# One written-out order of the calls on each engine of a two-layer sequence kernel, and its last batch without matmuls that nothing reads

## The reference, cut to what matters

```
# layer 0, per batch: linear attention over the context, then batch norm and a residual
g, theta, phi = conv1x1(g_w, ctx), conv1x1(theta_w, x), conv1x1(phi_w, ctx)
y = (theta^T phi / 512) g ;  x1 = bn(w_w y + w_b) + x
# layer 1, per batch: time mixing with a recurrence over 256 steps in 32 heads of 16
xa = ln(x1);  sx = shift(xa) - xa;  five mixes xw, xk, xv, xr, xg through low-rank tanh
w = exp(-exp(time_decay + tanh(xw d1) d2));  r, k, v = xr Wr^T, xk Wk^T, xv Wv^T;  g = silu(xg Wg^T)
s_new = k v^T + w * s;   out = r (faaaa * k v^T + s)      # step by step in time
x2 = x1 + (groupnorm(out) * g) Wo^T
# then channel mixing
xc = ln(x2); xk2, xr2 from xc and its shift
out = x2 + sigmoid(xr2 fWr^T) * (square(relu(xk2 fWk^T)) fWv^T)
```

## Time and profile before

| what | value |
|---|---|
| median of three runs | 872.42 us (869.52 to 874.44) |
| span of the profiled execution | 871.9 us |
| PE matmul busy | 813.5 us, 93% |
| VectorE busy | 602.6 us, 69% |
| ScalarE busy | 354.4 us, 41% |
| GpSimd busy | 295.4 us, 34% |
| mean granted TensorE clock | 0.986 |

### The profile page before, as it was taken

One profiled execution on the slowest core, in us unless ns is written; L12 is line 12 of the kernel. 1 busy time (PEld: TensorE's weight loads), 2 busy tenths in 40 slices (PEclk: granted clock), 3 DMA queues, 4 the chain that ended last, 5 costly groups with the idle time before them and its releaser, 6 DMA issues.

```text
span 871.9 us, 18035 instructions
## 1 busy us (share of the span) xinstructions
PE 813.5 (93%) x7370; PEld 543.0 (62%) x7370; DVE 602.6 (69%) x1110; ACT 354.4 (41%) x715; POOL 295.4 (34%) x281
## 2 busy tenths in 40 slices
PE   6799999799989999899998999899998899999997
PEld 4577568457754676457773677546764377456674
DVE  1484966996589836996389945898369876893441
ACT  1322336524552427324454155524174156225422
POOL 2043741474028410474007620284104821640000
PEclk9899999999999999999999999999999899999999
DMA  9830103000010001100011001200002000100000
GB/s 300 327 97 1 49 2 123 1 2 2 26 49 2 1 26 49 49 1 2 26 49 50 1 3 51 71 1 2 2 2 73 0 3 2 49 1 3 25 25 24
DMA packets 17026, 34.20 MB, mean 39 GB/s; under 512 B 2224, under 2 KB 3888, under 8 KB 16944
## 3 DMA queue, kind: packets, MB, share of 16 engines
q1 hardware_dynamic: 14048, 31.20, 10.5%
q10 hardware_dynamic: 2896, 1.86, 0.7%
HBM read 24.66 MB, written 8.39 MB: 38 GB/s over the span
## 4 chain that ended last, share of the span: by engine, by line
PE 75%; DVE 12%; issue 6%; ACT 4%; POOL 2%; DMA 1%; DVEq 0%; ACTq 0%; POOLq 0%
PE PB L528 24%; PE PC L535 13%; PE CH L624 5%; PE PC L528 4%; PE CH L682 3%; DVE xmix L1565 3%; PE PC L717 3%; PE CH L661 3%; PE PB L379 3%; DVE av L1659 2%; PE PA L402 2%; PE PA L509 2%; PE PB L489 2%; PE CH L468 2%; POOL xmix L2057 1%
## 5 line engine op out<-in xcount | busy, mean ns | idle before, releaser
L2057 POOL TENSOR_TENSOR xmix<-xmix,xa 128x512 f32<-128x512 f32 x80 | 94.0, 1195 | 166.9 <-DVE xmix L1565 166.9
L2070 POOL TENSOR_TENSOR prod<-RA,K 128x512 f32<-128x512 f32 x112 | 127.2, 1161 | 23.7 <-DVE RA L1629 20.9
L1238 ACT ACTIVATE st<-av,half 32x512 f32<-32x512 f32 x64 | 74.7, 1167 | 44.5 <-DVE av L1712 43.1
L624 PE MATMUL CH<-prod,ones 32*32 32x512 f32 (+1 forms) x1152 | 75.8, 582 | 13.8 <-DVE av L1659 8.9
L1565 DVE SCALAR_TENSOR_TENSOR xmix<-PA,chan,sx 128x256 f32<-128x256 f32 x128 | 52.9, 475 | 39.0 <-PE PA L509 37.4
L1659 DVE TENSOR_TENSOR av<-CH,vT 128x512 f32<-128x512 f32 x112 | 71.7, 681 | 10.5 <-PE CH L624 10.3
L1670 DVE TENSOR_REDUCE yred<-av 128x64 f32<-128x512 f32 (+2 forms) x112 | 70.9, 674 | 0.0
L717 PE MATMUL PC<-sq_Wo,y 128*128 128x512 f32 x128 | 62.6, 621 | 6.8 <-DVE y L1755 6.8
L2082 POOL TENSOR_TENSOR K<-K,W 128x512 f32<-128x512 f32 x8 | 15.3, 1914 | 143.4 <-DVE prod L1595 143.4
L528 PE MATMUL PB<-xmix,sq_Wk 128*128 128x256 f32 x256 | 61.7, 386 | 0.0
L535 PE MATMUL PC<-sq_fWr,sxc 128*128 128x512 f32 x128 | 60.4, 612 | 0.0
(11 more groups left out here) (163 smaller groups left out, 1388.5 us busy)
## 6 DMA issues: line engine op xcount, KB each, us to landing
x<-x_rows SPq DMA_DIRECT2D x11, 512.0 KB, 3.4
x<-in_x SPq DMA_DIRECT2D x8, 512.0 KB, 3.9
x_rows<-x SPq DMA_DIRECT2D x8, 512.0 KB, 4.7
out_x<-x SPq DMA_DIRECT2D x8, 512.0 KB, 2.8
ctx_t<-in_ctx SPq DMA_DIRECT2D x5, 512.0 KB, 3.8
y<-in_ctx SPq DMA_DIRECT2D x3, 512.0 KB, 8.4
sq_Wk<-in_square SPq DMA_DIRECT2D x1, 1024.0 KB, 13.6
sq_Wv<-in_square SPq DMA_DIRECT2D x1, 1024.0 KB, 16.7
```

Of the source, the lines that this page charges most:

```text
L624: mm = pe.matmul(out, ones16[rows, rows], v, start=True, stop=True)
L1238: act.activation(st[p, :, :, 32 * q:32 * q + S], src, ACT.Copy, scale=half[p, 0:1]).then_inc(st_ready, 1)
L2057: pool.tensor_tensor(m, m, xa[:, ct:ct + 2, 1:L + 1], ALU.add).then_inc(mix_ready, 1)
L2070: pool.tensor_tensor(by_pair(prod[:, g % 4, :], h), r, k, ALU.mult).then_inc(prod_pool, 1)
```

## The change

The three functions `fill`, `iteration` and `drain` of each engine become one function `program()` that lists every call with its batch numbers. `batch`, `first` and the tests for `None` go. The instructions inside each call stay the same, except that all the calls of `keep_warm(PB, n)` and the waits on `gate_ready` ahead of them are gone. The four warm-up matmuls ahead of everything stay. On no engine is a call of another kind added or removed; their order is new, and no longer the same from batch to batch. The diff, cut to what the next sections speak of:

```diff
             def b_sums(u, t):
-                if u == B - 1:
-                    pe.wait_ge(gate_ready, 2 * B)
-                    keep_warm(PB, 4)
...
             def b_reads(u, t):
                 turn_values(yint, t)
-                if u == B - 1:
-                    pe.wait_ge(gate_ready, 2 * B)
-                    keep_warm(PB, 8)
...
             def c_turn_y(c, t):
-                if c == B - 1 and t == 0:
-                    pe.wait_ge(gate_ready, 2 * B)
-                    keep_warm(PB, 5)
```

`c_wo`, `c_turn` and `c_key` lose the same lines with 7, 9 and 11. The first calls of PE:

```diff
-            def fill():
+            def program():
                 a_phi_g(0, 0)
-                setup(0)
                 a_phi_g(0, 1)
                 a_att(0)
+                setup(0)
                 a_theta(0)
...
                 a_theta(1)
+                a_ranks(0)
                 a_wa(1)
-                a_ranks(0)
                 a_x1(1)
```

PE from the reads of batch 2 to the turned keys of batch 3, in place of `iteration(5)`:

```diff
+                b_reads(2, 0)
+                a_gate(3, 1)
+                a_turn(4)
+                a_gate(3, 2)
+                a_gate(3, 3)
+                b_reads(2, 1)
+                c_receptance(1, 0, 1)
+                a_ranks(4)
+                c_receptance(1, 1, 0)
+                c_receptance(1, 1, 1)
+                b_chunks(3, 0, 2)
+                c_value(1, 0, 0)
+                b_chunks(3, 2, 3)
+                a_first_mixes(4)
+                c_value(1, 0, 1)
+                c_value(1, 1, 0)
+                c_value(1, 1, 1)
+                c_turn_y(2, 0)
+                a_mix(4, 2)
+                c_turn_y(2, 1)
+                b_chunks(3, 3, 5)
+                a_decay(4)
+                c_wo(2, 0, 0)
+                c_wo(2, 0, 1)
+                c_wo(2, 1, 0)
+                c_wo(2, 1, 1)
+                a_decay2(4)
+                b_chunks(3, 5, 7)
+                a_key(4, 0)
+                b_chunks(3, 7, 9)
+                a_key(4, 1)
+                a_key(4, 2)
+                b_chunks(3, 9, 11)
+                c_turn(2, 0)
+                c_turn(2, 1)
+                a_mix(4, 3)
+                a_key(4, 3)
+                b_chunks(3, 11, 13)
+                c_key(2, 0)
+                c_key(2, 1)
+                b_chunks(3, 13, 15)
+                c_key(2, 2)
+                b_chunks(3, 15, 17)
+                c_key(2, 3)
+                b_turn_k(3)
```

PE between the second sums and the first reads of batch 4:

```diff
+                b_sums(4, 1)
...
+                a_value(5, 3)
+                c_receptance(3, 0, 1)
+                c_receptance(3, 1, 0)
+                a_theta(6)
+                a_receptance(5, 0)
+                c_receptance(3, 1, 1)
+                b_reads(4, 0)
```

PE in the chunk stages of batch 1 and of batch 6, and at the reads of batch 7:

```diff
+                b_chunks(1, 2, 3)
+                b_chunks(1, 3, 5)
+                a_mix(2, 2)
...
+                b_chunks(6, 9, 11)
                 b_chunks(6, 11, 13)
-                a_key(7, 1)
+                a_mix(7, 3)
                 b_chunks(6, 13, 17)
...
                 c_receptance(6, 1, 0)
+                c_receptance(6, 1, 1)
                 b_reads(7, 0)
-                c_receptance(6, 1, 1)
+                c_value(6, 0, 0)
                 b_reads(7, 1)
-                c_value(6, 0, 0)
```

ACT, at the start and in the last batch:

```diff
                 a_theta(0)
-                setup(0)
                 a_xa(0)
...
                 a_xa(1)
+                setup(0)
                 a_gate(0)
...
-                b_square(7, 0)
+                c_sig(6)
                 b_expand(7, 1, 0)
                 b_expand(7, 1, 1)
                 b_expand(7, 1, 2)
                 b_expand(7, 1, 3)
-                c_sig(6)
+                b_square(7, 0)
                 b_square(7, 1)
```

DVE at the start, and around the chunk stage of batch 4 (in place of `iteration(6)`):

```diff
+                a_phi_g(0)
                 scale_output_weights(0)
-                a_phi_g(0)
                 turn_output_weights(0)
                 a_wa(0)
                 a_x1(0)
-                a_phi_g(1)
                 a_stats(0)
                 a_z(0)
+                a_phi_g(1)
                 a_shift(0)
...
+                b_wprod(4)
+                b_prod(4, 0)
+                b_prod(4, 1)
+                b_normed(3, 0)
+                b_normed(3, 1)
+                a_gate(4)
+                b_chunks(4, 0, 2)
+                c_out(2, 0)
+                a_mix(5, 0)
+                a_mix(5, 1)
+                b_chunks(4, 2, 3)
+                c_out(2, 1)
+                c_gate(3, 0)
+                a_mix(5, 2)
+                c_gate(3, 1)
+                b_chunks(4, 3, 5)
+                b_chunks(4, 5, 9)
+                c_x2(3, 0)
+                c_x2(3, 1)
+                c_z(3, 0)
+                b_chunks(4, 9, 11)
+                c_z(3, 1)
+                a_mix(5, 3)
+                c_shift(3)
+                c_shift_r(3)
+                b_chunks(4, 11, 13)
+                a_mix(5, 4)
+                b_chunks(4, 13, 17)
```

More of the change, by code:

```diff
@@ new lines, in program @@
+                a_mix(2, 3)
+                c_key(0, 0)
+                c_key(0, 1)
+                b_chunks(1, 15, 17)
+                c_key(0, 2)
+                b_turn_k(1)
+                c_key(0, 3)
+                b_turn_v(1)
+                a_mix(2, 4)
+                a_value(2, 0)
+                b_sums(1, 0)
+                a_value(2, 1)
+                a_turn(3)
+                b_sums(1, 1)
+                a_value(2, 2)
+                a_value(2, 3)
+                c_receptance(0, 0, 0)
@@ new lines, in program @@
+                c_key(1, 3)
+                b_turn_v(2)
+                a_mix(3, 4)
+                a_value(3, 0)
+                b_sums(2, 0)
+                a_phi_g(4, 0)
+                a_phi_g(4, 1)
+                b_sums(2, 1)
+                a_att(4)
+                a_value(3, 1)
+                a_value(3, 2)
+                a_theta(4)
+                c_receptance(1, 0, 0)
+                a_wa(4)
+                a_value(3, 3)
+                a_x1(4)
+                a_receptance(3, 0)
@@ new lines, in program @@
+                b_turn_k(3)
+                a_mix(4, 4)
+                b_turn_v(3)
+                a_value(4, 0)
+                a_phi_g(5, 0)
+                a_phi_g(5, 1)
+                b_sums(3, 0)
+                a_att(5)
+                a_theta(5)
+                a_wa(5)
+                b_sums(3, 1)
+                a_value(4, 1)
+                a_value(4, 2)
+                a_value(4, 3)
+                a_receptance(4, 0)
+                a_receptance(4, 1)
+                c_receptance(2, 0, 0)
@@ new lines, in program @@
+                a_phi_g(7, 1)
+                b_turn_k(5)
+                c_key(4, 3)
+                b_turn_v(5)
+                a_value(6, 0)
+                a_value(6, 1)
+                a_theta(7)
+                b_sums(5, 0)
+                a_att(7)
+                a_value(6, 2)
+                a_value(6, 3)
+                b_sums(5, 1)
+                a_wa(7)
+                c_receptance(4, 0, 0)
+                c_receptance(4, 0, 1)
+                c_receptance(4, 1, 0)
+                c_receptance(4, 1, 1)
@@ L1468, in drain @@
                 c_sig(7)
-            fill()
-            for i in range(3, 8):
-                iteration(i)
-            drain()
+            program()
         @block.vector
@@ new lines, in program @@
+                a_mix(3, 2)
+                c_z(1, 1)
+                b_chunks(2, 9, 11)
+                b_chunks(2, 11, 13)
+                c_shift(1)
+                b_chunks(2, 13, 17)
+                a_mix(3, 3)
+                a_mix(3, 4)
+                b_sums(2, 0)
+                a_phi_g(4)
+                b_wprod(3)
+                b_sums(2, 1)
+                b_scan(2)
+                c_shift_r(1)
+                a_wa(4)
+                b_expand(2, 0)
+                a_x1(4)
@@ new lines, in program @@
+                c_x2(4, 1)
+                a_mix(6, 2)
+                b_chunks(5, 5, 9)
+                c_z(4, 0)
+                c_z(4, 1)
+                b_chunks(5, 9, 11)
+                b_chunks(5, 11, 13)
+                a_mix(6, 3)
+                c_shift(4)
+                c_shift_r(4)
+                a_mix(6, 4)
+                b_chunks(5, 13, 17)
+                b_wprod(6)
+                a_phi_g(7)
+                b_sums(5, 0)
+                b_sums(5, 1)
+                a_wa(7)
```

1198 lines of the change are left out of this document (717 added, 481 removed).

## The result

The changed kernel takes 866.70 us (median of 6 runs, 865.41 to 870.83), the kernel before in the same job 873.69 us (6 runs): a ratio of 0.9933 with a 95% interval of [0.9911, 0.9955]. It is faster by 0.7% where 2.8% were forecast, and lies just above the range of 830 to 866. Executions that took far longer than the rest (1187, 2093 and 2761 us) are left out of all ratios here; `order_with_kw` and `start_old_rest` were profiled in such a one, so no timeline of theirs is read.

What follows compares the result with a forecast made beforehand. PE was taken as the bound, busy 813.5 of 871.9 us, with only its 58.4 idle us and the clock open to change. Terms -8 - 14.6 + 3 - 10 + 5.8 = -23.8 gave 848 us (840 to 856; wider range 830 to 866).

Steps and rivals of the forecast that it cites:

- Part 1: The start: reordered calls cover two PE waits and bring the transpose 7.2 us earlier; -8 us, ends 3.4 and 14.65.
- Part 3: Stages between the chunk stages: no idle time to lose, less cover for the states' chain; 0.5 us per batch, +3.
- Part 2: Six chunk stages: PE work moved in cuts idle time from 33.6 to 19 us; -14.6, ends 0 and -21.6.
- built alike: Chunk stages of batches 2, 4 and 5: expected, like batch 3's, to keep some 2 us of uncovered waits each.
- idle for idle: Rival: work moved into the chunk stages makes DVE the bound again, Parts 2 and 3 give nothing; 860 us, chance 0.15.
- Part 4: Last batch: removing unread matmuls gives about 6 us and the order about 4; gross -10, ends -6 and -25.5.
- the clock: Last batch: PE idling before `c_wo` and `c_key` makes the clock fall twice, 2.9 us each; +5.8.
- about 15: Sign in the tail: about 15 us of PE idle time expected where there was 1.
- The price of a fall: Time lost per clock fall, from three calls near 677.60 us taking 6.86 rather than about 4 us: 2.9 us.
- Cold last batch: Rival: the clock falls before `c_wo` and stays at 1.2 GHz, so no change; 871 us, chance 0.07.
- cover runs out: Slower rival: five batches wait about 7.8 us each for the states, 39 us in all; 884 us, chance 0.11.
- The rule on the clock that was weighed: Skill rule cited for the last batch: idle stretches between bursts throttle the array again; by it Part 4 is -4.2, without it -10.

Runs made afterwards that it cites:

- order_with_kw: The changed kernel's new order with all 56 unread matmuls of the last batch put back: 871.16 us, 0.9989 of the kernel before.
- start_old_rest: The kernel before with the new start, the context of batch 2 loaded early and no unread matmuls, old order elsewhere: 857.91 us, 0.9844.
- the paired runs: new_mid_kw2 against old_mid_kw2, run in one job and differing only in the order of middle and tail: 857.06 and 856.73 us.
- ctx_early: The changed kernel with batch 2's context and the store of batch 0's x1 issued ahead of the last four weight loads: 861.01 us, 0.9874.
- new_mid_kw2: ctx_early with two groups of unread matmuls put back, ahead of c_turn and c_key of the last batch: 857.06 us, 0.9822 of the kernel before.
- old_mid_kw2: start_old_rest with two groups of unread matmuls kept, ahead of c_turn and c_key of the last batch: 856.73 us, 0.9821 of the kernel before.

## Why the prediction was wrong, point by point

- **Part 1 (-8, measured 0).** This is one of the two steps that failed. The chain was read right to 0.1 us (transpose 7.1 us earlier, 7.2 predicted), and the gain by itself is 9.9 us. What failed is the step from "the transpose comes 7.2 us earlier" to the term -8, as if that much came off the end of the start: nothing was named that is late next. Part 3 looked at SP's queue for the later loads, but the load of the context of batch 2, whose reader `a_phi_g(2, 0)` moves from 43.27 to 34.6 us, was not among them. The runs show a wait of 6.60 us for it and half clock behind the wait, in place of the 8 us.
- **Part 2 (-14.6) and Part 3 (+3), together -11.6, measured -1.7 in the trace and 0 in the paired runs.** This is the other, and the larger. Most of the idle time that they forecast was saved: 8.0 us in the changed kernel, 11.2 in the pair, and Part 3's extra waits for the states did not come (in the changed kernel PE waited for `st` in batch 7 alone). Batches 2 and 3 came to 1.7 us; batches 4 and 5, said to be "built alike", stopped at 4.1 and 4.7. What failed is the step that let an idle microsecond saved be a microsecond of time, with durations taken from the old order: the instructions that stayed became longer, by 6.3 us in the changed kernel and 11.2 in the pair. The clock, which the prediction charged only in the last batch, fell more often in the new middle (7.7 us in the pair, 8.1 in the changed kernel against 4.8 in the kernel before), and `c_shift` slowed beside GpSimd.
- **The rival "idle for idle" (860, chance 0.15)** named the right outcome for Parts 2 and 3, nothing, with the wrong mechanism: DVE did not take the idle time back in the stages of batches 2 and 3, though it does bound batch 1's. PE's idle time fell, and its busy time rose.
- **Part 4 and the clock (-10 + 5.8 = -4.2).** The sum came close, 4.1 us in the runs (0.9953 of 871.8) and 6.9 in the trace of the tail, but its parts did not, so this is in part luck. The removal was put at -6 and the clock at +5.8, which leaves 0.2 for what measured 4.1; the order was put at -4, and the traces give it 0.1. The 25.5 us of unread matmuls less 15.6 us of new idle time ("about 15" was said) make a gross of 9.9 from the removal alone. The clock cost 3.8 us in the changed kernel, at the first reads and `c_key` and not at `c_wo`, and some 9 in the tail of `ctx_early`; 5.8 lies between.
- **The price of a fall** was read with a slip: x4 is one part of `c_wo` and not two. The three calls take 1.09 + 1.09 + 1.98 = 4.2 us at full clock, so 2.7 us were lost and not 2.9, which changes nothing.
- **"Cold last batch" and "cover runs out"** did not happen: the clock came back each time (in a long fall, 155 to 170 us of new_mid_kw2, (1 - clock) x length is 5.15 us, or 10.3 us at 1.2 GHz), and PE never waited for the states of batches 1 to 6.
- **The rule on the clock that was weighed** (the Trainium skill, "TensorE: Matmul & The Clock Gate", section "HAM oscillation") was charged against the removal. The runs say that it bore on the order as well: order_with_kw has all the unread matmuls and still a mean clock of 0.982 against 0.990, with the late load's wait in it.

What stays open: which waits make the clock fall. A wait of 3.26 us went with a fall in the kernel before and with none in old_mid_kw2, in the same call. Why the old order has its two middle falls in four traces and none in three is open too. And the split of the middle's loss between clock and VectorE rests on the traces' sums; the runs only bound it.

The best kernels are new_mid_kw2 and old_mid_kw2, 1.8% faster than the kernel before and 1.1% faster than the changed one. The second keeps the old order of the middle and the tail.

## What to carry to other kernels

When a chain is shortened, list every reader that moves forward and the transfer that it reads with its place in the issuing queue, not only the engines' calls: one load cost here all that a new start had gained. An idle microsecond saved on a busy engine is not yet a microsecond: take PE's instructions as equal in number over an equal stretch and compare busy time and granted clock before crediting it. To judge a rewritten order, put its parts (start, middle, tail) one by one on the old order; the sum of a mixed kernel hides which part gives what.

## What the runs showed of the hardware

- The granted clock of one and the same kernel moves between executions. Of six runs of old_mid_kw2 the fastest took 854.03 us at a mean clock of 0.998, the slowest 860.12 at 0.988: some 0.6 us for each 0.001. Half a per cent of a PE-bound kernel can be nothing but this.
- More idle time can go with a higher clock: in the same 723.7 us, 40.9 us of idle time in 47 waits with no fall (`old_mid_kw2`), 29.7 us in 38 waits with three falls (`new_mid_kw2`). The longest waits are 3.26 and 3.41 us.
- VectorE instructions of 128 x 256 with two inputs in SBUF took 480 ns in the kernel before and up to 1485 ns beside GpSimd in the changed one; one with an input in PSUM took 475 in both.
- A context of 512 KB took 14 us from issue to use behind eight weight loads of 1 MB (changed kernel). Five contexts of the same size, of batch 0 and of batches 4 to 7, land 3.8 us after their issue (median, kernel before).
